# Causal attention scores of a Trainium2 kernel: one true-fp32 matmul against a block-diagonal q, or four rounded-fp32 matmuls from stacked high and low parts

## What is computed

```python
q = (h_in @ wq).reshape(B, S, H, dqk)      # H = 8 heads, dqk = 32
k = (h_in @ wk).reshape(B, S, H, dqk)
Dmat = Fcum[..., :, None] - Fcum[..., None, :] + i_pre[..., None, :]   # causal, -inf above
Smat = exp(Dmat - max(Dmat))
qk = einsum('bhsd,bhtd->bhst', q, k) / sqrt(dqk)
C = qk * Smat
h = einsum('bhst,bhtd->bhsd', C / n, v)
```

## Time and profile before

| | us |
|---|---|
| median of three executions | 2475.16 (2471.98 to 2475.67) |
| the profiled execution, its own time | 2471.92 |
| its span, first to last instruction | 2470.1 |
| PE busy with matmuls | 2416.0, 98% |
| DVE, ACT, POOL busy | 1253.8, 914.9, 610.8 |
| 16 DMA engines, mean share of the span | 58.8%, 508.34 MB moved |

### The profile page before, as it was taken

One profiled execution on the slowest core, in us unless ns is written; L12 is line 12 of the kernel. 1 busy time (PEld: TensorE's weight loads), 2 busy tenths in 40 slices (PEclk: granted clock), 3 DMA queues, 4 the chain that ended last, 5 costly groups with the idle time before them and its releaser, 6 DMA issues. The chain is left out here.

```text
span 2470.1 us, 33080 instructions
## 1 busy us (share of the span) xinstructions
PE 2416.0 (98%) x11376; PEld 1947.6 (79%) x11376; DVE 1253.8 (51%) x2205; ACT 914.9 (37%) x1683; POOL 610.8 (25%) x499
## 2 busy tenths in 40 slices
PE   7999999999999999999999999999999999999998
PEld 5677787787787778778777877888888888888887
DVE  6776536765773675577367557743222222222222
ACT  5433245355454535545443544554111111111111
POOL 2346523221321322232132223222111111111111
PEclk9999999999999999999999999999999999999999
DMA  5055554473464448356444825676867867867865
GB/s 210 1 199 207 216 226 140 167 275 127 152 213 182 154 166 281 107 172 208 167 162 165 293 102 174 208 265 223 279 237 273 282 241 260 296 241 255 287 221 198
DMA packets 115513, 508.34 MB, mean 206 GB/s; under 512 B 11120, under 2 KB 11120, under 8 KB 80144
## 3 DMA queue, kind: packets, MB, share of 16 engines
q1 hardware_dynamic: 110016, 496.46, 57.2%
q10 hardware_dynamic: 5328, 9.70, 1.3%
HBM read 417.39 MB, written 87.69 MB: 204 GB/s over the span
## 5 line engine op out<-in xcount | busy, mean ns | idle before, releaser
L747 PE MATMUL up_bank<-act_hi,gud 128*128 128x512 f32 x1728 | 591.8, 403 | 0.0
L747 PE MATMUL gate_bank<-act_hi,gud 128*128 128x512 f32 x1728 | 574.7, 393 | 2.7 <-DVE th L1587 2.7
L2073 POOL TENSOR_TENSOR hidden_lo<-hm,hidden_hi 128x512 fp32r<-128x512 f32 x216 | 281.9, 1305 | 1136.3 <-ACT hidden_hi L1131 1136.3
L947 PE MATMUL acc<-gud,hidden_hi 128*128 128x512 f32 x1728 | 436.2, 394 | 0.9 <-ACT hidden_hi L1131 0.9
L1587 DVE SCALAR_TENSOR_TENSOR th<-th,gate_bank 128x512 f32<-128x512 f32 x216 | 147.9, 685 | 514.3 <-ACT th L1126 514.2
L1131 ACT ACTIVATE hidden_hi<-hm 128x512 fp32r<-128x512 f32 x216 | 135.9, 629 | 692.6 <-PE acc L950 681.2
L747 PEld LDWEIGHTS up_bank<-act_hi,gud 128*128 128x128 f32 x1728 | 324.6, 188 | 81.0 <-issue 13.5
L747 PEld LDWEIGHTS gate_bank<-act_hi,gud 128*128 128x128 f32 x1728 | 324.3, 188 | 75.1 <-DVE th L1587 4.6
L947 PEld LDWEIGHTS acc<-gud,hidden_hi 128*128 128x128 f32 x1728 | 319.5, 188 | 68.1 <-issue 4.2
L747 PE MATMUL up_bank<-act_lo,gud 128*128 128x512 f32 x864 | 337.7, 391 | 0.0
L747 PE MATMUL gate_bank<-act_lo,gud 128*128 128x512 f32 x864 | 336.7, 390 | 0.0
(11 more groups left out here) (326 smaller groups left out, 2973.0 us busy)
## 6 DMA issues: line engine op xcount, KB each, us to landing
gud<-mlp_parts SPq DMA_DIRECT2D x112, 1024.0 KB, 5.1
gud<-ghost_parts SPq DMA_DIRECT2D x88, 1024.0 KB, 5.9
gud<-mlp_parts SPq DMA_DIRECT2D x112, 512.0 KB, 3.9
gud<-ghost_parts SPq DMA_DIRECT2D x88, 512.0 KB, 4.6
ghost_parts<-look_w SPq DMA_DIRECT2D x35, 512.0 KB, 3.8
mlp_parts<-gud SPq DMA_DIRECT2D x16, 1024.0 KB, 3.9
vo_w_hi<-vo_parts SPq DMA_DIRECT2D x13, 1024.0 KB, 7.1
vo_w_lo<-vo_parts SPq DMA_DIRECT2D x13, 1024.0 KB, 9.9
```

Of the source, the lines that this page charges most:

```text
L747: mm = pe.matmul(dst, l[a], r[c], start=first and k == 0 and n == 0, stop=last and k == len(lhs) - 1 and n == 2)
L947: pe.matmul(ACC[i][:], HH[0][:, toks(i)], W3[:, z, 2, n, :], start=t == 0 and n == 0, stop=False)
L2073: pool.tensor_tensor(HH[1][:], hm[:], HH[0][:].bitcast(f32), ALU.subtract).then_inc(of.low.sem, 1)
```

## The change

Scores are computed from one stationary and one moving tile of 96 rows per head, the three products stacked along the rows: rows 0 to 31 hold q high against k high, 32 to 63 q high against k low, 64 to 95 q low against k high. Four matmuls per unit (one per head, 128 moving columns, fp32r) take the place of the one with 512 columns. The parts reach that layout through device memory: ACT writes the high parts of `GB` to a tile `stack` (two buffers, by i % 2) and a plain copy of q to `qT`, DVE writes the low parts (`qkT_lo`), SP stores both parts of each chunk (`store_qk`, 2 DMAs of 256 KB) and loads each unit's 96 rows (`load_qk`, 6 DMAs of 64 KB with runs of 512 bytes) into the same tile `stack`. `qbd` is no longer made, except for the first block, which keeps the old way. `q_k_T(i)` waits for DVE's low part of chunk i-1 as well; ACT's `qkT_(i)` waits, for i >= 2, until the stores of chunk i-2 have landed.

```diff
+        qk_parts = nc.dram_tensor("qk_parts", (4, NB, P, G * P), f32, kind="Internal").ap()
-        qkT = sb("qkT", [P, 2, G, TOK])
+        qT = sb("qT", [P, G, TOK])
+        stack = sb("stack", [P, 2, 2, HG * P], f32r)
...
+        def stacked(at, chunks):
+            return at[0] * (HALVES * NB * 16) + ((at[1] - 1) * NB // 2 + chunks) * 32
+        def stack_loaded(at, u):
+            return at[0] * (HALVES * NB * 96) + ((at[1] - 1) * NB + u // 2 + 1) * 96
...
@@ SP @@
+            def store_qk(at, i):
+                wait(sp, vec_qkT, at, i, "lo")
+                for part in range(2):
+                    src = stack[:, i % 2, part, :].bitcast(f32).rearrange("p (z n) -> p z n", z=2)
+                    sp.dma_start(qk_parts[part::2, i].rearrange("z p n -> p z n"), src).then_inc(st_qk[i % 2], 16)
+            def load_qk(at, u):
+                i, g = u // G, u % G
+                if u < 2:
+                    sp.wait_ge(st_qk[u], stacked(at, NB // 2))
+                else:
+                    wait(sp, pe_unit, at, u - 2, "scores")
+                for r, parts in enumerate((slice(0, 3, 2), slice(0, 4, 3), slice(1, 3))):
+                    dst = stack[r * DQ:(r + 1) * DQ, u % 2, :, :].bitcast(f32).rearrange("d z (h n) -> d z h n", h=HG)
+                    src = qk_parts[parts, i, :, g * P:(g + 1) * P].rearrange("z (h d) n -> d z h n", h=HG)
+                    for z in range(2):
+                        sp.dma_start(dst[:, z], src[:, z]).then_inc(ld_qk[u % 2], 16)
...
@@ SP, behind store_xt(1, XH[1]) of the first block @@
+            for i in range(NB):
+                store_qk(SECOND, i)
+            for u in range(2):
+                load_qk(SECOND, u)
@@ SP, tiles(at) @@
                 for t in range(NM):
+                    if not here(at, TAIL) and 1 <= t < UNITS - 1:
+                        load_qk(at, t + 1)
...
                             store_xt(b * HALVES + half, XH[half])
+                            for i in range(NB):
+                                store_qk(at, i)
+                            for u in range(2):
+                                load_qk(at, u)
@@ PE, q_k_T @@
                 if i:
-                    wait(pe, act_qkT, at, i - 1, "k")
+                    wait(pe, act_qkT, at, i - 1, "done")
+                    if not here(at, FIRST):
+                        wait(pe, vec_qkT, at, i - 1, "lo")
@@ PE, unit_1, blocks other than the first @@
+                pe.wait_ge(ld_qk[u % 2], stack_loaded(at, u))
+                if u:
                     wait(pe, vec_unit, at, u - 1, "update")
-                pe.matmul(pick(at, u, B, ACC[1])[:], qkT_of(at)[:, 1, g, toks(j)], pick(at, u, qbd, qbd2)[:, :, :], start=True, stop=True)\
-                    .then_inc(pe_unit.sem, 1)
+                for h in range(HG):
+                    mm = pe.matmul(B[:, toks(h)], stack[0:3 * DQ, u % 2, 1, toks(h)], stack[0:3 * DQ, u % 2, 0, toks(h)],
+                                   start=True, stop=True)
+                mm.then_inc(pe_unit.sem, 1)
@@ PE, units_first order @@
+                unit_2(FIRST, u)
                 if 3 <= u < 7:
                     q_k_T(SECOND, u - 3)
-                unit_2(FIRST, u)
@@ ACT, qkT_, blocks other than the first @@
+                if i >= 2:
+                    act.wait_ge(st_qk[i % 2], stacked(at, i // 2))
+                act.activation(stack[:, i % 2, 0, :], GB[:], ACT.Copy).then_inc(act_qkT.sem, 1)
+                act.activation(qT[:, :, i * P:(i + 1) * P], both[:, 0], ACT.Copy).then_inc(act_qkT.sem, 1)
@@ ACT, tiles @@
-                if stage:
-                    qbd_(at, 0)
...
-                    if t + 1 < UNITS:
-                        qbd_(at, t + 1)
@@ DVE @@
+            def qkT_lo(at, i):
+                wait(dve, act_qkT, at, i, "done")
+                dve.tensor_tensor(stack[:, i % 2, 1, :], GB[:], stack[:, i % 2, 0, :].bitcast(f32), ALU.subtract)\
+                    .then_inc(vec_qkT.sem, 1)
@@ DVE, front @@
                 else:
+                    qkT_lo(at, 0)
+                    qkT_lo(at, 1)
                     dve.wait_ge(st_mlp[1 - at[1]], at[0] * 16)
                 gate_sum(at)
+                if not here(at, FIRST):
+                    qkT_lo(at, 2)
                 gate_maxima(at)
+                if not here(at, FIRST):
+                    qkT_lo(at, 3)
                 gate_factors(at)
@@ DVE, units_first @@
                     weights(at, u)
+                    if u in (4, 5, 6, 7):
+                        qkT_lo(SECOND, u - 4)
```

More of the change, by code:

```diff
@@ L267, in kn_, with qT_of @@
             return kn_first if here(at, FIRST) else kn
-        def qkT_of(at):
-            return qkT_first if here(at, FIRST) else qkT
+        def qT_of(at):
+            return qkT_first[:, 0, :, :] if here(at, FIRST) else qT
         qkT_first = first_rows[:, 8:12, :].rearrange("p (z g) n -> p z g n", z=2)
@@ L317, in program @@
         st_vo = sem("st_vo")
+        st_qk = [sem(f"st_qk{i}") for i in range(2)]
+        ld_qk = [sem(f"ld_qk{i}") for i in range(2)]
         ld_idx = [sem(f"ld_idx{i}") for i in range(2)]
@@ L352, in program @@
         act_qk = Steps(sem("act_qk"), NB, ["q", "k"])
-        act_qkT = Steps(sem("act_qkT"), NB, ["q", "k"])
+        act_qkT = Steps(sem("act_qkT"), NB, ["part", "done"])
         act_v = Steps(sem("act_v"), NB, ["done"])
@@ L364, in program @@
         vec_o = Steps(sem("vec_o"), NB, ["done"])
+        vec_qkT = Steps(sem("vec_qkT"), NB, ["lo"], credit=-NB)
         vec_unit = FirstAhead(sem("vec_unit"), UNITS, ["masked", "weights", "before", "heads", "update", "state"], 1)
@@ L817, in unit_1 @@
                     .then_inc(pe_unit.sem, 1)
-                wait(pe, act_qbd, at, u, "h3")
-                wait(pe, act_qkT, at, NB - 1, "k")
                 if here(at, FIRST):
+                    wait(pe, act_qbd, at, u, "h3")
+                    wait(pe, act_qkT, at, NB - 1, "done")
                     if u >= 2:
                         wait(pe, vec_unit, at, u - 2, "update")
-                elif u:
+                    pe.matmul(pick(at, u, B, ACC[1])[:], qkT_first[:, 1, g, toks(j)], pick(at, u, qbd, qbd2)[:, :, :],
+                              start=True, stop=True).then_inc(pe_unit.sem, 1)
+                    return
+                pe.wait_ge(ld_qk[u % 2], stack_loaded(at, u))
+                if u:
                     wait(pe, vec_unit, at, u - 1, "update")
-                pe.matmul(pick(at, u, B, ACC[1])[:], qkT_of(at)[:, 1, g, toks(j)], pick(at, u, qbd, qbd2)[:, :, :], start=True, stop=True)\
-                    .then_inc(pe_unit.sem, 1)
+                for h in range(HG):
+                    mm = pe.matmul(B[:, toks(h)], stack[0:3 * DQ, u % 2, 1, toks(h)], stack[0:3 * DQ, u % 2, 0, toks(h)],
+                                   start=True, stop=True)
+                mm.then_inc(pe_unit.sem, 1)
             def unit_2(at, u):
@@ L832, in unit_2 @@
                     wait(pe, vec_unit, at, u - 2, "state")
-                pe.matmul(pick(at, u, B, ACC[1])[:, 0:HG * VS], qkT_of(at)[:, 0, g, toks(j)], kv[:, g, :, :], start=True, stop=True)
+                pe.matmul(pick(at, u, B, ACC[1])[:, 0:HG * VS], qT_of(at)[:, g, toks(j)], kv[:, g, :, :], start=True, stop=True)
                 for h in range(HG):
@@ L856, in ho_T @@
                 else:
-                    wait(pe, act_qkT, SECOND, NB - 1, "k")
+                    wait(pe, act_qkT, SECOND, NB - 1, "done")
+                    wait(pe, vec_qkT, SECOND, NB - 1, "lo")
                 f = hn[:, :, :].rearrange("p h d -> p (h d)")
@@ L907, in gate @@
                 if t == 0 and stage:
-                    wait(pe, act_qkT, stage, NB - 1, "k")
+                    wait(pe, act_qkT, stage, NB - 1, "done")
+                    wait(pe, vec_qkT, stage, NB - 1, "lo")
                 else:
@@ L1277, in qkT_ @@
                 wait(act, pe_qkT, at, i)
[L1278 to L1281, removed]
+                both = GB[:, :].rearrange("p (z g n) -> p z g n", z=2, g=G)
+                if here(at, FIRST):
+                    for z in range(2):
+                        act.activation(qkT_first[:, z, :, i * P:(i + 1) * P], both[:, z], ACT.Copy).then_inc(act_qkT.sem, 1)
+                    return
+                if i >= 2:
+                    act.wait_ge(st_qk[i % 2], stacked(at, i // 2))
+                act.activation(stack[:, i % 2, 0, :], GB[:], ACT.Copy).then_inc(act_qkT.sem, 1)
+                act.activation(qT[:, :, i * P:(i + 1) * P], both[:, 0], ACT.Copy).then_inc(act_qkT.sem, 1)
             def v(at, i):
@@ L1335, in qbd_ @@
                 j, g = u // G, u % G
[L1336 to L1343, removed]
+                if u >= 2:
+                    wait(act, pe_unit, at, u - 2, "scores")
+                wait(act, act_qkT, at, j, "part")
                 for h in range(HG):
-                    act.activation(pick(at, u, qbd, qbd2)[:, h, :], qkT_of(at)[:, 0, g, j * P:(j + 1) * P], ACT.Copy,
```

(5 more changed lines are left out.)

## The result

Before: 2474.44 us, median of 4 runs (2471.98 to 2475.67). After: 2500.41 us, median of 4 (2498.52 to 2502.32). The ratio is 1.0106 with a 95% interval of 1.0089 to 1.0124: slower by 26 us, where 33 were forecast. The profiled execution took 2498.52 us, with a span of 2496.6 and a mean granted clock of PE of 0.987 of full (before: 2470.1 and 0.995).

The account below looks back on a forecast made before the run. PE, busy 98% of the span, was taken to bound the kernel. Scores -24.6, holes +42.0, clock +15.0 and first blocks -0.3 gave +32.1 on 2471.92, or 2504.0; 3 more for the median made 2507 us, range 2488 to 2543.

Parts of the forecast that it names:

- Price of the scores: Tiles with units: four narrow matmuls cost 0.41 us like four transposes, against 0.85 before; 56 units gain 24.6 us.
- Rival A: Score matmuls: 128 rounded columns go at true fp32's pace, so four still cost 0.85 us; 2532 us, chance 0.35.
- The hole: Six loop fronts: ACT's copy of chunk 2 waits for chunk 0's stores, so PE stands 7.0 us each, 42.0 in all.
- its upper bound of 8.6: Hole per front if the 1 KB runs of the chunk stores go at half the rate: 8.6 us.
- The clock: PE behind each front's hole: lower granted clock adds 2.5 us per front, bounds 1.6 and 3.4, 15.0 in all.
- The first blocks: First block's DVE subtractions and the second block's lost wait for `qbd`: together -0.3 us, bounds -1 and +3.
- The hole needs only FIFO service on one queue: SP's queue in the fronts: chunk 0's stores land behind the xt stores issued before them; hole given chance 0.9.
- The other ground: Fronts: DMA engines are full until the last xt store lands, share 1.03 in 777 to 779, 0.28 in 779 to 781.
- rival B: Fronts: chunk 0's stores overtake or are served between the xt stores' pieces, no hole opens; 2452 us, chance 0.07.
- ACT, DVE and SP in the tiles: Tiles: ACT's copies and DVE's subtractions hide beside PE, SP's six loads per unit cost zero, bounds 0 to 1 us.

Follow-up runs that it names:

- experiment 7: Changed kernel with the two xt stores and the second vo weight reload issued behind the stores of chunks 0 and 1, blocks 2 to 7: 2450.73 us.
- experiment 9: Changed kernel with the four narrow score matmuls of each unit of blocks 2 to 8 issued twice, 224 more matmuls: 2521.67 us.
- experiment 4: Changed kernel with the four narrow score matmuls of each unit read as true fp32 instead of the rounded type: 2520.65 us, one run.
- experiment 6: Changed kernel with only the second 1 MB xt store moved behind the stores of chunks 0 and 1, the first left ahead: 2487.11 us.
- experiment 1: Changed kernel with both 1 MB xt stores moved behind the stores of chunks 0 and 1 on SP's queue, blocks 2 to 7: 2456.67 us.
- experiment 2: Kernel before, with only a wait added: ACT's copy of chunk 2 waits for the xt stores in the loop's six fronts: 2513.14 us, one run.
- experiment 5: Changed kernel with the stores of chunks 0 and 1 issued by ACT on its own queue, the rest on SP in old order: 2500.07 us.

## Why the prediction held, point by point

The forecast was 2507 us in a range of 2488 to 2543, slower with 0.88; it came to 2500.4. The mechanism stands where it was put. All four terms of the sum were off by some us, and one reason was wrong. In the traces the holes came out 4.4 us below the forecast and the clock 4.3 below, the scores 1.6 and the first blocks 1.5 above: +26.5 in place of +32.1. So a part of the nearness is that the errors cancel.

**Price of the scores: 24.6 forecast, 22.1 and 23.0 measured** in the tiles of the two traces without and with a hole (experiment 7 and the changed kernel). The step that took 0.103 us per matmul from the transposes held: by experiment 9 one more costs 0.095 to 0.100. From `MX,AL` to the second matmul of `up` (880.36 to 881.27) are now 0.91 us, which leaves 0.91 - 0.47 = 0.44 for the four against 0.85 before: 0.41 per unit in place of 0.44, and 56 times 0.41 is 23.0. The Trainium skill's 81 ns per pair (TensorE: Matmul & The Clock Gate, Back-to-back issue gap) would have made it 0.32 for the four, an estimate from that page; the runs show 0.38 to 0.44, and they decide. Rival A fell with that, and experiment 4 shows what it would have cost: 20 us.

**The hole: 7.0 forecast, 6.4 measured** in block (2, 0), 6.3 on average (37.6 us over six fronts for 42.0). Counted from the block's first mark, every time of the forecast can be laid beside the trace: xt store issued at +11.5 (now +11.6), last landing at +26.2 (+25.8), ACT's copy at +27.5 (+27.1), PE's transposes at +29.3 (+28.7). Chunk 0's second store lands 1.3 us behind the last xt store (790.7 and 789.5), which is the forecast's 0.5 MB at 2.5 us per MB; so nothing shows the half rate that its upper bound of 8.6 rests on, and by its own terms that bound would be 7.0 + 1.3 = 8.3. The landing came 0.4 us sooner, and the hand-over from ACT through DVE to PE took 1.65 us, not 1.8. That all six fronts are alike held: ACT's six waits are 6.6 us on average, 7.1 at most.

**The clock: 2.5 a front forecast, 1.4 measured in block (2, 0), 1.8 on average.** Hole and clock together make 7.8 us in block (2, 0), which is what its front grew by, and 48.3 us over six fronts where 57.0 were forecast; less the holes' 37.6 this leaves 10.7 for 15.0. The step that was mis-sized is "the new hole is longer than both, so I add 2.5": it supposes that a longer hole costs at least as much, and experiment 6 shows no such order. What can be read from the windows is that half clock inside a hole costs nothing: the mean over the hole is 0.68 in block (2, 0) of the changed kernel and 0.86 in the same block of experiment 6, so in the first the clock had been down for longer before PE had anything to do. What decides when it falls, these traces don't show.

**The first blocks: -0.3 forecast, +1.2 in the trace of after.** The first front is 1.6 us longer and the second 0.4 shorter. The profile shows where the 1.6 are: soon after PE's first matmul the changed kernel's trace has 3.4 us of half clock, and the trace of before has none there. That of before has such a stretch in the second front, which the changed kernel's trace hasn't. First the changed kernel, then the two of the kernel before (columns as in rows 10):

```profile
17.10:20.50 3.40, 3.40 (x10) 1.96 (x8) 3.31 (x9) 0.34 (x1) 0.00 (x0) 0.50 0.58 189
```

```profile
17.10:20.50 3.40, 3.40 (x17) 2.43 (x16) 3.31 (x9) 0.33 (x1) 0.00 (x0) 1.00 0.54 171
141.00:144.40 3.40, 3.40 (x10) 2.65 (x9) 2.75 (x6) 0.00 (x0) 2.10 (x2) 0.50 0.81 305
```

It is not the change: experiment 1, which has all of it, has no such stretch there and a first front no longer than before, while experiment 2, which has none of the change, is 1.0 us longer there and 1.5 us behind when the loop starts. It differs from trace to trace, and with one trace of each kernel nothing tells how often it comes.

**The reason that was wrong** is "The hole needs only FIFO service on one queue". By experiment 5 it needs no common queue: the engines' backlog is enough. The other ground, which stands against rival B, engines full until the last landing, carried the forecast. Had the change put its stores on ACT's queue, my rival B would have been the natural forecast, and wrong by 48 us.

**ACT, DVE and SP in the tiles cost nothing,** as forecast: with the hole removed (experiment 7) all stretches with units are shorter by what the scores save. The loads of 64 KB land in 2.0 us by the median of 336, and no instruction waits for one.

**Rival B's number came true by another way.** In the changed kernel no store overtook; with SP's order changed there was no hole, and the time is 2450.7 where B said 2452.

## What to carry to other kernels

Before a short transfer that something waits for is put into a stage, list the bytes that are issued ahead of it on all queues and divide by the rate that the windows show; here another queue didn't help while the engines were full, and another order did. When stores are moved back, follow each source buffer to its next writer, not only each destination to its reader. A gain per unit and a loss per block are to be summed apart: here the order of four large DMAs decided the sign of a change whose arithmetic was sound.

## What the runs showed that I had not expected

- Small stores on an otherwise empty queue waited for the engines as if they stood behind the large ones: 256 KB took 10 to 11 us to land at a DMA share of 0.96 to 1.00, against a median of 2.9 us over all 56 in the changed kernel.
- The clock's loss did not shrink with the hole: six holes of 5.8 to 6.8 us (37.6 in all) had 23.0 us of half clock behind them, six of 3.4 to 4.5 us (23.1 in all) had 25.1, and six of 0.9 to 1.8 us had none. Taking 2.4 us off each hole won 2.0 us a front; removing the hole won all 8.0.
- A rounded matmul of 96 rows and 128 moving columns costs 0.095 to 0.11 us, half of the 0.21 us (0.85/4) that true fp32 takes for the same columns; for 512 columns it is 0.237 against 0.85.
